# Graph network on one core: 384-node accumulation banks, one-hots made by ScalarE, and an eighth stretch of pass 1 without gathers

## The reference, cut to what matters

```python
def gcn_conv(x, src, dst, ew, W, b):            # twice, with self-loops (weight 1) added
    deg = segment_sum(ew, dst, num_segments=n)
    dinv = where(deg > 0, rsqrt(deg), 0.0)
    h = x @ W
    msg = h[src] * (dinv[src] * ew * dinv[dst])[:, None]
    return segment_sum(msg, dst, num_segments=n) + b
h = relu(gcn_conv(x, ..., W1, b1));  h = sigmoid(gcn_conv(h, ..., W2, b2))
x = layernorm(x + h)
# attention
z = x @ fc_w.T;  rh = edge_attr @ fc_r_w.T
e = leaky(z[src] @ aw[0] + z[dst] @ aw[1] + rh @ aw[2])
alpha = exp(e - segment_max(e)) / segment_sum(exp(...))
out = relu(segment_sum(alpha[:, None] * (z[src] + rh)) + z @ loop_w)
x = layernorm(x + out)
```

## Time and profile before

| what | value |
|---|---|
| median of 3 runs | 2682.67 us (2680.21 to 2683.11) |
| profiled execution, its own time | 2688.04 us |
| its span, first to last instruction | 2686.2 us |
| busy: PE / DVE / ACT / POOL | 1962.5 / 1731.3 / 253.3 / 1998.3 us |
| TensorE clock granted, mean | 0.813 of full speed |
| gathers: pass 0 / 1 / 2 | 622 / 558 / 782 |

### The profile page before, as it was taken

One profiled execution on the slowest core, in us unless ns is written; L12 is line 12 of the kernel. 1 busy time (PEld: TensorE's weight loads), 2 busy tenths in 40 slices (PEclk: granted clock), 3 DMA queues, 4 the chain that ended last, 5 costly groups with the idle time before them and its releaser, 6 DMA issues.

```text
span 2686.2 us, 39490 instructions
## 1 busy us (share of the span) xinstructions
PE 1962.5 (73%) x13505; PEld 1689.4 (63%) x13505; DVE 1731.3 (64%) x7072; ACT 253.3 (9%) x444; POOL 1998.3 (74%) x1973
## 2 busy tenths in 40 slices
PE   5777888989896787979797884466457566567558
PEld 4567767777785565757575763366456556456557
DVE  8989976867764456665656564556556457556465
ACT  0010000101100011101111111000000000000000
POOL 7777777777776777777777774777777777777772
PEclk9659888989986889889878885678788777788777
DMA  4243222222224233343424334644444444444441
GB/s 133 57 118 96 64 70 65 77 63 77 69 65 126 63 83 115 89 123 91 117 78 116 89 107 138 173 116 114 106 113 114 103 114 106 113 114 106 103 104 33
DMA packets 251443, 263.33 MB, mean 98 GB/s; under 512 B 41630, under 2 KB 195765, under 8 KB 251222
## 3 DMA queue, kind: packets, MB, share of 16 engines
q0 software_dynamic: 62784, 130.31, 19.8%
q1 hardware_dynamic: 175214, 123.97, 15.8%
q10 hardware_dynamic: 13240, 6.45, 0.8%
HBM read 247.25 MB, written 13.72 MB: 97 GB/s over the span
## 4 chain that ended last, share of the span: by engine, by line
POOL 45%; issue 19%; PE 16%; DVE 11%; DMA 7%; SPq 1%; ACT 0%; POOLq 0%; DVEq 0%; ACTq 0%
POOL ring L562 45%; PE ps L694 7%; DMA ring<-x_d,srcC 5%; DVE SR L1226 5%; PE ps L749 5%; DVE SR L1257 2%; PE ps L697 1%; DMA ring<-h_d,srcC 1%; PE ps L737 1%; DMA U<-dlo_d 1%; PE ps L679 1%; SPq L400 1%; SPq L482 1%; PE ps L634 0%; DVE SR L1323 0%
## 5 line engine op out<-in xcount | busy, mean ns | idle before, releaser
L562 POOL DMA_INDIRECT ring<-x_d,srcC x1260 | 1262.1, 1002 | 411.4 <-issue 395.2
L694 PE MATMUL ps<-SR,ring 128*128 128x128 f32 (+9 forms) x5076 | 904.3, 311 | 203.1 <-DVE SR L1257 75.3
L694 PEld LDWEIGHTS ps<-SR,ring 128*128 128x128 f32 x5076 | 797.9, 227 | 231.8 <-issue 140.5
L562 POOL DMA_INDIRECT ring<-h_d,srcC x558 | 593.5, 1064 | 183.1 <-issue 175.5
L749 PE MATMUL ps<-SR 128*128 128x376 f32 x1176 | 430.2, 518 | 33.6 <-ACT SR L989 33.6
L697 PE MATMUL ps<-SR 128*128 128x128 f32 (+10 forms) x1948 | 427.4, 305 | 0.0
L697 PEld LDWEIGHTS ps<-SR 128*128 128x128 f32 x1948 | 348.8, 224 | 0.0
L749 PEld LDWEIGHTS ps<-SR 128*128 128x128 f32 x1176 | 233.5, 207 | 176.1 <-ACT SR L989 35.4
L1323 DVE TENSOR_SCALAR SR<-iota_s,cols 128x376 f32<-128x376 f32 x588 | 246.7, 473 | 67.8 <-PE ps L749 67.5
L1257 DVE TENSOR_SCALAR SR<-iota_s,rankC,ewC 128x128 f32<-128x128 f32 x1036 | 280.0, 363 | 0.3
L829 PE MATMUL ps<-ident,cols 128*32 128x128 f32 (+2 forms) x78 | 20.4, 396 | 316.5 <-DVE cols L1533 316.5
(11 more groups left out here) (226 smaller groups left out, 1721.3 us busy)
## 6 DMA issues: line engine op xcount, KB each, us to landing
SR<-in_edge_attr_dram SPq DMA_DIRECT2D x97, 512.0 KB, 4.2
U<-dlo_d SPq DMA_DIRECT2D x98, 256.0 KB, 3.5
ring<-x_d,srcC POOLq DMA_INDIRECT x1260
SR<-low_d SPq DMA_DIRECT2D x72, 256.0 KB, 3.3
ring<-h_d,srcC POOLq DMA_INDIRECT x558
U<-lo_d SPq DMA_DIRECT2D x18, 256.0 KB, 3.2
x_d<-U SPq DMA_DIRECT2D x12, 264.0 KB, 4.5
rows<-x_d SPq DMA_DIRECT2D x12, 264.0 KB
```

The costliest lines, as they stand in the source:

```text
L562: pool.indirect_dma_start(ring[:, gg % R, k, 0:width], None, (x if p == 0 and h < R0 else table)[:, :], bass.IndirectOffsetOnAxis(ap=srcC[ ...
L694: last = nc.tensor.matmul(ps[(p * NK + k) % 2][:, lo:hi], ring[:, gg % R, j, 0:D], S[:, gg % NS, j, w0:w0 + hi - lo], start=False, stop=t ...
```

## The change

**Banks of 384 nodes.** In passes 0 and 1 a bank now belongs to 3 blocks (`BA = 384`, `NA = 17` banks, the last of one block) but its accumulator is still 512 columns wide. Every tile lies whole in one accumulator (`bank_of`, `column`), and the last 128 columns, which belong to the next bank, are added to that bank by one matmul with the identity when the bank is copied out (in `layer`). No tile is split in passes 0 and 1. Pass 2 keeps its 512-node banks. `FIRST`/`LAST` stay for pass 2; `blocks(k)`, `NK` become `home(k)`, `NA` elsewhere.

**One-hots by ScalarE.** The one-hots of lookups and picks are two dependent activations, `relu(1 - |x - p|)`, the first in place. They stand in ACT's order, in the step where DVE had them.

**An eighth run.** Pass 1 has 8 runs without gathers: 32 tiles fewer are gathered there, and its steps are 66 instead of 70. The 104 chunks of pass 1 are spread over 61 steps. The tables of the 8 sets are made every 7 steps in pass 0 instead of every 8. ACT's order in a step of pass 1 is now: copies, one-hots of chunks, then `squash`.

```diff
-SETK = (5, 7, 9, 10, 11, 1, 3)
-USED = ((0, 1, 2, 3, 4), (5, 6, 0, 1, 2, 3, 4))
+BA = 3 * P
+NA = -(-NP // BA)
+def bank_of(t):
+    return max((GT * t - 2 * (W // 4)) // BA, 0) if t >= GT else 0
+def home(k):
+    return range(k * BA // P, min((k + 1) * BA // P, NB))
+def column(t):
+    return base(t) - bank_of(t) * BA
+OPENS = [min(t for t in range(T) if bank_of(t) == k) for k in range(NA)]
+CLOSES = [max(t for t in range(T) if bank_of(t) == k) // GT for k in range(NA)]
+SETK = (8, 10, 12, 14, 15, 2, 4, 6)
+USED = ((0, 1, 2, 3, 4), (5, 6, 7, 0, 1, 2, 3, 4))
-CUT = [[30, 39, 48, 57, 66], [1, 10, 19, 29, 38, 47, 57]]
-MAKE = [18 + 8 * i for i in range(NSET)]
+CHUNK_AT = [[30 + 9 * (m // NC) + m % NC * 9 // NC for m in range(N0 * NC)],
+            [1 + m * 61 // (len(USED[1]) * NC) for m in range(len(USED[1]) * NC)]]
+MAKE = [18 + 7 * i for i in range(NSET)]
+MAKE_STEP = (0, 2, 4, 5)
...
@@ sum_group
+                    if p < 2:
+                        k = bank_of(t)
+                        if t == OPENS[k] and k + 1 < NA:
+                            open_bank(p, k)
+                        last = nc.tensor.matmul(ps[(p * NA + k) % 2][:, column(t):column(t) + W], ring[:, gg % R, j, 0:D],
+                                                S[:, gg % NS, j, :], start=False, stop=t + 1 in OPENS or t + 1 == T)
+                        continue
...
@@ layer
+                if k + 2 == NA:
+                    open_bank(p, NA - 1)
+                if k + 1 < NA:
+                    nc.tensor.matmul(ps[(gb + 1) % 2][:, 0:BW - BA], ident[:, :], aggT[:, gb % 2, BA:BW], start=False, stop=False)
...
@@ scalar
+            def one_hot(out, low):
+                apart[0] += 1
+                nc.scalar.activation(low, low, ACT.Abs, bias=negp[:, 0:1]).then_inc(s("low_apart"), 1)
+                act.wait_ge(s("low_apart"), apart[0])
+                return nc.scalar.activation(out, low, ACT.Relu, bias=negp[:, 1:2], scale=-1.0)
+            def slot_onehot(m):
+                ...
+                one_hot(ohS[:, m % 2, 0:w], loS[:, n % 2, c:c + w]).then_inc(s("oh_made"), 1)
+            def begin_pick(q):
+                ...
+                one_hot(ohD[:, q % 2, :], dloB[:, q % 2, :]).then_inc(s("ohd_made"), 1)
             for h in range(HS[1]):
-                for k in range(NK - 2):
+                set_copies(1, h)
+                for m in chunks_at(1, h):
+                    slot_onehot(m)
+                for k in range(NA - 2):
                     if CLOSEH[1][k] == h - 2:
                         squash(k)
-                set_copies(1, h)
...
+                for q in picks_at(h):
+                    begin_pick(q)
...
@@ vector, make_slots
-                v.tensor_scalar(ohS[:, m % 2, 0:w_], loS[:, n_ % 2, c:c + w_], pidx[:, 0:1], None, ALU.is_equal).then_inc(s("oh_made"), 1)
-            def begin_pick(q):
-                v.tensor_scalar(ohD[:, q % 2, :], dloB[:, q % 2, :], pidx[:, 0:1], None, ALU.is_equal).then_inc(s("ohd_made"), 1)
```

204 lines of the change are left out of this document (107 added, 97 removed).

## The result

The changed kernel takes 2643.95 us median (2638.93 to 2647.20, 4 runs) and the kernel before, in the same comparison, 2682.89 us. The ratio is 0.9859 [0.9841, 0.9877], 39 us less. Forecast were 2597 us with a range of 2578 to 2640. The sign was right, and the time lies just outside the range.

What follows compares the result with a forecast made beforehand. POOL's gathers were taken to bound the kernel; -40.0 (fewer gathers), -34 (less stretch), -9.5 and -2 (seams) gave -85.5 us, span 2600.7, profiled execution 2602.5, and a median of 2597 us, range 2578 to 2640.

Steps and rivals of the forecast that it cites:

- What bounds the kernel: Whole kernel: POOL's gathers end to end, 1.25 us each plus stretch, with two seams waiting for tables, and a tail.
- part 1: Pass 1's gathers: 32 fewer at 1.25 us each, -40.0 us, all on the path while POOL bounds.
- Part 2: Gathers held by DVE's bursts: moving one-hots to ScalarE shortens them, net -34 us, ends 0 and -55.
- shared by busy time: Gathers' 152 us of stretch split by DVE's wide operations: 118 of 365 us leaves, so at most 49 us goes.
- Rival C: Gathers stay held by DVE's remaining bursts: +8 us instead of -34, time 2639 us; chance 0.12.
- Part 3: POOL's waits between passes, without split tiles: second seam -9.5 us (ends 0 and -13), first seam -2 us.
- Part 4: Work of PE and ACT in pass 1 stays hidden behind POOL's gathers: 670 us against POOL's 693.
- So I let POOL keep its lead: Pass 1: POOL still sets the pace, 10.5 us a step, despite ACT's one-hots; no loss entered the sum.
- 0.93 of my count: Pass 1's chain: the count before gave 790 us against 736 at most; scaled likewise, 720 becomes 670 us.
- The four bare steps let PE come back by up to 20 us: End of pass 1: last chunks end at step 61 of 66, so PE regains up to 20 us afterwards.
- Rival A: ACT's and PE's chain paces pass 1 at 11.3 us a step: second seam 30 us longer, 2627 us; chance 0.17.
- Pass 2 and the tail are as before: After pass 1's gathers: later picks add nothing on the path, so no change, 0 us.

Runs made afterwards that it cites:

- e4: The changed kernel with seven runs in pass 1, the eighth taken out and chunks spread over 65 steps; 2667.31 us.
- f3: The kernel before with the 384-node banks alone, but set tables made every 7 steps as in the changed kernel; 2664.79 us.
- e3: The changed kernel with all one-hots, of lookups and picks, made by VectorE again; 2638.31 us.
- e1: The changed kernel with the picks' one-hots made by VectorE again, the lookups' staying on ScalarE; 2652.00 us.
- e2: The changed kernel with the lookups' one-hots made by VectorE again, the picks' staying on ScalarE; 2623.78 us.
- h2: The changed kernel with one more wait on VectorE: a chunk's slot matrices wait for the lookup two chunks back; 2638.01 us.
- f2: The changed kernel with ScalarE's copy of a finished set issued behind the step's one-hots, `squash` and picks; 2632.02 us.
- f1: The changed kernel with no picks handed out in steps that hold a `squash`; 2634.32 us.
- h3: e2 with each lookup's one-hot made twice on VectorE, 156 operations more; 2643.82 us.

## Why the prediction was right or wrong, point by point

- **What bounds the kernel, and part 1**: right. 526 gathers instead of 558 at 1.25 us are the -40.0 us in full. What the eighth run brings in all is less, 23 us (e4) or 26 (f3, e3), because a seam grows with it. PE's busy time in pass 1, which "stays near 630", fell to 579 us, at a granted clock of 0.89 instead of 0.84.
- **Part 2, the size**: half right. The direction and the mechanism (a burst holds a gather) stand, but not "shared by busy time". The picks' one-hots, the shorter line with 44.4 us of busy time, bring the whole gain (20 to 26 us by e1, e2 and e3, 11 to 16 at equal lag); the lookups' one-hots with 73.7 us bring none (e2). The gathers of x gained nothing; the forecast's -34 was 13 us too much, as -20.8 was measured. Rival C, "the stretch stays", is right for pass 0. Whether the gathers of x are stretched more when ScalarE makes the lookups' one-hots (7 us on average) stays open; h2 took up one reason and couldn't settle it.
- **Part 3**: right in itself for the second seam. The banks alone shorten it by 8.0 us (f3; 9.5 was forecast). The first seam gave 6.6 in f3, with the tables made earlier, and 4.9 in the changed kernel (2 was forecast).
- **Part 4 is the step that failed**: "So I let POOL keep its lead." It put no growth of the lag into the sum, and the second seam came 14.5 us longer instead of 9.5 shorter: 24 of the 39 us by which the sum is off. The prices were right: a half one-hot takes 0.72 and 1.14 us (0.71 and 1.14 forecast), so the 10.4 us of a full step needn't change. What was wrong is the `squash` step. I priced it at +5 us, in half the banks, and took as a gain that the copies come ahead of it. The trace shows 22.1 us from sum to sum behind step 16 and 12.0 to 17.2 behind the others after which the lag jumps, against 10.3 on average behind the rest. Three things make such a step, not all of them each time. The copy of the finished set waits for PE's slot sums and holds up one-hots that don't need it (f2). Two table loads of 1.28 us, one of them hidden in ACT's idle time before, are on the chain in the timeline; no run prices them. And two picks wait behind it all (f1). The sum of a pass's work against POOL's 693 us, "0.93 of my count", could not show this: what one long step loses, steps of 10 give back only slowly when POOL needs 10.7. (Its items make 7.2 us a bank, where 7.5 stands, and 7.5 x 17 is 127.5, not 125; neither changes the result.)
- **"The four bare steps let PE come back by up to 20 us"**: they gave back next to nothing (lag 28.7 us at step 61, 31.2 at 63, 28.5 at the end), because S waits there behind `squash` and `end_pick`.
- **Rival A** named this outcome: the chain paces pass 1. Its step of 11.3 us was near (11.2 on average from step 16 to 63), it gave the seam 30 us more (14.5 came) and the time 2627. A and half of C together are what happened; they were priced apart. The range took in each of them, but not both. Rival A had a chance of 0.17, and nothing in the forecast's sum stood for it.
- **The tail**: "Pass 2 and the tail are as before" was 4.4 us off. It is 45.4 to 50.5 us over the runs, and wasn't followed up.

Of the Trainium skill's two rules, the one on VectorE's operations and GpSimd's port (SBUF — State Buffer, Who interferes with whom) fits the picks' one-hots, by which the gathers of pass 1 lost 11 to 26 us of stretch. That no hold came back on ScalarE isn't shown, with the gathers of x as they are. That the lookups' one-hots brought nothing when moved (e2), and that less was held when they were doubled (h3), the rule alone doesn't give. The other (ScalarE: Activation LUTs, Rules for kernel authors), by which `relu`, `max` and `add` belong on VectorE, is half borne out: the lookups' one-hots are better there (e2: 0.9791 against 0.9859), the picks' are not (e3: 2638.3 us against e2's 2623.8).

## What to carry to other kernels

When work goes to an engine with much idle time, don't ask how busy it gets but what stands in its order in the fullest step: write that step out, with every wait and every table load, and see who is held behind it. An idle engine hides its waits only until something urgent stands behind them; moving one copy that waits to the end of the step, or the urgent work into another step, took 16 to 28 us from a seam here, though part of it came back elsewhere and only 10 to 12 us show in the medians. A gain at one place of the chain is not yet a gain in time. And undo each part of a change by itself: the best kernel keeps two parts and half of the third.

## What the runs showed of the hardware that was not expected

- A gather (0.94 us undisturbed) beside VectorE's bursts can be held to the burst's end (3.10 us at 1295.02) or hardly at all (0.94, 1.18 beside a burst as long). With 156 operations more on VectorE none of pass 1 lasted over 2 us (h3: 999 ns on average against e2's 1029); that kernel's PE also lagged 32.6 us instead of 8.2 at the end of the pass. Gathers without such operations beside them aren't held (944 ns on average in 335).
- An activation with a pointer operand over 1024 columns took 1.15 us, over 512 columns 0.72, back to back, without a gap for the dependence of the second half on the first beyond 0.03 to 0.04 us. The estimate from 128 columns (0.15 us for the pointer, 0.83 ns a column) held at both widths.
- Chips differ: the same kernel took 2681 to 2684 us where the runs of the table were made and 3590 to 3625 us on two others; the cause isn't known.
